# POOL waits at every eighth gather of a graph attention until the gathers before it have landed

## The reference, cut to what matters

```python
h = (x_flat @ W_gat).reshape(M, HEADS, NUM_EXPERTS)          # 4 heads x 4 experts
a_src = (h * att_src).sum(-1)
a_dst = (h * att_dst).sum(-1)
e = leaky_relu(a_src[src] + a_dst[dst], negative_slope=0.2)
ee = exp(e - segment_max(e, dst)[dst])
denom = segment_sum(ee, dst)
agg = segment_sum(h[src] * (ee / denom[dst])[:, :, None], dst) + b_gat
scores = _layernorm(agg, ln_gamma, ln_beta).reshape(M, HEADS, NUM_EXPERTS).mean(1)
topk_s, topk_i = top_k(scores, 2)
w = softmax(topk_s)
out = sum over ei of gate(ei) * (gelu(x @ W1[ei] + b1[ei]) @ W2[ei] + b2[ei])
```

## Time and profile before

| | |
|---|---|
| timed runs | 4308.76, 4301.39 and 4308.22 us, median 4308.22 us |
| profiled execution | span 4665.5 us from the first to the last instruction; no time of its own is given beside it |
| PE busy | 3696.0 us (79%) |
| DVE busy | 2192.7 us (47%) |
| ACT busy | 1348.5 us (29%) |
| POOL busy | 739.5 us (16%) |
| mean granted clock of PE | 0.886 |

### The profile page before, as it was taken

The page is one execution under the profiler, slowest core; times in us unless marked ns, Lnnn a source line. Parts: engine busy times, 40 slices in busy tenths (PEclk is TensorE's granted clock), DMA queues, the critical chain, the costliest instruction groups (busy, mean ns, idle before and its releaser), DMA issues. The chain is left out here.

```text
span 4665.5 us, 90783 instructions
## 1 busy us (share of the span) xinstructions
PE 3696.0 (79%) x23366; PEld 2634.7 (56%) x23367; DVE 2192.7 (47%) x5709; ACT 1348.5 (29%) x2983; POOL 739.5 (16%) x1224
## 2 busy tenths in 40 slices
PE   4888864899699989973464629859989899789998
PEld 2444433566388579651354416539879544457776
DVE  7888878888700221151263420270130677723333
ACT  2555532677700110320010203240000135233333
POOL 3222100000000000017423470200000466100000
PEclk9999975887799899986787859879999999989999
DMA  2111220323244024102010121224425100010000
GB/s 105 47 74 74 93 86 0 91 90 90 76 160 157 32 108 184 60 16 53 11 53 4 40 25 39 98 77 170 165 105 196 49 1 1 5 29 7 13 13 27
DMA packets 125733, 317.98 MB, mean 68 GB/s; under 512 B 43522, under 2 KB 76785, under 8 KB 111116
## 3 DMA queue, kind: packets, MB, share of 16 engines
q1 hardware_dynamic: 110404, 300.31, 18.5%
q0 software_dynamic: 11808, 9.68, 1.5%
q10 hardware_dynamic: 3404, 6.53, 0.4%
HBM read 244.21 MB, written 72.41 MB: 68 GB/s over the span
## 5 line engine op out<-in xcount | busy, mean ns | idle before, releaser
L554 PE MATMUL ps<-hot_key,hot_src 128*126 128x512 bf16 (+1 forms) x2208 | 416.9, 314 | 38.6 <-DVE hot_key L519 21.1
L519 DVE TENSOR_SCALAR hot_key<-col_iota,run_keys 128x625 bf16<-128x625 int16 x1104 | 393.7, 378 | 0.0
L2441 PE MATMUL ps<-xnT,ew 128*128 (+2 forms) x640 | 207.5, 479 | 206.7 <-issue 150.9
L1335 PE MATMUL ps<-gnn_u_thirds,near 125*128 125x256 bf16 x3000 | 334.7, 274 | 23.1 <-issue 23.1
L554 PEld LDWEIGHTS ps<-hot_key,hot_src 128*126 128x126 bf16 x2208 | 212.7, 136 | 234.2 <-DVE hot_key L519 171.7
L1335 PEld LDWEIGHTS ps<-gnn_u_thirds,near 125*128 125x128 bf16 x3000 | 329.7, 141 | 26.3 <-issue 24.7
L2441 PEld LDWEIGHTS ps<-xnT,ew 128*128 128x128 f32 x640 | 129.7, 210 | 279.2 <-issue 183.5
L2322 POOL DMA_INDIRECT rows_room<-node_table,src_idx x256 | 260.1, 1016 | 142.4 <-issue 142.4
L516 DVE TENSOR_SCALAR hot_src<-col_iota,run_srcs 128x125 bf16<-128x125 int16 x828 | 211.6, 256 | 97.4 <-PE ps L554 52.8
L863 PE MATMUL ps<-row_hot,slot_hot 128*128 128x512 f16 x1088 | 217.6, 351 | 3.1 <-DVE row_hot L1076 2.6
L2477 PE MATMUL ps<-table_thirds,rows_room 125*128 125x144 bf16 x1728 | 129.2, 232 | 113.9 <-issue 78.0
(11 more groups left out here) (570 smaller groups left out, 6651.9 us busy)
## 6 DMA issues: line engine op xcount, KB each, us to landing
near<-adjacency SPq DMA_DIRECT2D x80, 1562.5 KB, 6.6
adjacency<-counts SPq DMA_DIRECT2D x125, 312.5 KB, 2.2
own_in<-own_rows SPq DMA_DIRECT2D x34, 512.0 KB, 4.0
expert_rows<-rows_y SPq DMA_DIRECT2D x75, 125.0 KB
rows_room<-expert_rows SPq DMA_DIRECT2D x25, 375.0 KB
pair_in<-high_rows SPq DMA_DIRECT2D x34, 256.0 KB
pair_in<-low_rows SPq DMA_DIRECT2D x34, 256.0 KB
agg0a_adj<-adjacency SPq DMA_DIRECT2D x5, 1562.5 KB, 9.4
```

Of the source, the lines that this page charges most:

```text
L519: nc.vector.tensor_scalar(hot_key[:, j, :], col_iota[:], run_keys[:, ds(at, 1), j:j + 1].rearrange("p a j -> p (a j)"), None, ALU.is_equal ...
L554: last = nc.tensor.matmul(sums[:, b:e], hot_src[:, j, :], hot_key[:, j, b:e], start=False, stop=True, skip_group_check=True)
L1335: last = nc.tensor.matmul(ps[:, j, 0:width], lead_tiles[BUF[j]][:, k, :], parts.thirds[:, k, i, :], start=(k == 0 and i == 0), stop=(k == ...
L2441: last = nc.tensor.matmul(ps[:, piece % 2, 0:n], w1[i][:, c, m * 128:(m + 1) * 128], xnT[:, c, ds(g * NG + first, n)], start=(c == 0), sto ...
```

## The change

In `gather_rows`, ahead of every eighth gather of a call, POOL waits until all gathers that it has issued so far into this buffer have landed: 16 for each gather, plus what earlier blocks in the same buffer have added (`landed_before`). A buffer's very first gather (slot 96 in blocks 0 and 1, slot 0 in the others) is left out. The gathers, their order and everything else stay.

```diff
+                        def start_of(q):
+                            return TURNED if q < 2 else 0
+
+                        def landed_before(b, q):
+
+                            return 0 if q < 2 else (b - q) * (8 * SLOTS)
+
                         def gather_rows(b, q, first, stop):
 
                             alone(pool, idx_ready, b + 1)
                             for j in range(first, stop):
+                                if (j - first) % FEW == 0 and j > start_of(q):
+                                    alone(pool, got[q], landed_before(b, q) + 16 * (j - start_of(q)))
                                 pool.indirect_dma_start(
                                     out=fetched[q][:, j, :], out_offset=None, in_=node_table,
                                     in_offset=bass.IndirectOffsetOnAxis(ap=src_idx[:, q, j:j + 1], axis=0),
```

## The result

The kernel before takes 4308.49 us (median of four runs; one of them, 6012.78 us, is left out of the comparison), the changed kernel 4375.19 us (4373.02 to 4381.57, four runs). The ratio of the comparison is 1.017, 95% interval 1.0158 to 1.0182: slower by under 2%, but clear of the noise. The profiled execution of the changed kernel is one of its timed runs, 4376.03 us with a span of 4374.3, so here the profile may be read for the time. That of before had a span of 4665.5 us.

What follows compares the result with a forecast made beforehand. The profile's slow issue beside POOL's gathers was taken as absent from timed runs, leaving POOL's chain almost bare at `weigh_last`. Waits of 59 us less 4 of cover added 55 to 4308: 4363 us, range 4306 to 4405.

Steps and rivals of the forecast that it cites:

- the sum: POOL's chain of gathers: 59 us added by the waits, less 4 us of cover, so ACT stands 55 us.
- The premise: Beside POOL's gathers: the profile's 385.9 us lost to slow issue on PE are hardly present in the timed runs.
- rival "faster": Beside the gathers: slow issue is in timed runs too and pauses give the others room; down to 4280 us, chance 0.10.
- 28.6 us: Rest left unexplained, around or elsewhere in the span: 4279.6 us without the losses against the timed median of 4308.2.
- The price of a wait: POOL ahead of every eighth gather: 1.8 us per bare wait, 32 bare, 59 us in all (43 to 111).
- POOL's chain end at 2550: POOL's gathers before the change, rebuilt without the losses: chain ends at 2550 us, with 16 us for stretched gathers.
- rival "dearer": POOL's waits: landings slow down beside stores of expert rows, 3.23 us a wait; 4415 us, chance 0.08.
- The cover: At `weigh_last` on ACT: PE's side at 2566.9 against block 3's `exp_in` at 2563 hides 4 us of waiting.
- my bound of 20: At `weigh_last`: cover of POOL's chain is 20 us if gathers are not stretched by DVE's work.
- PE's clean arrival: At `weigh_last` in expert 2's last run: PE's side arrives at 2566.9 without the 365.0 us lost before.
- the case's own range: Whole kernel: the forecast's main case, chance 0.70, lies between 4331 and 4400 us.
- The signs: Profile after: POOL's gaps 2.1 us at 36 places, span falling while timed runs rise; wrong if the timed median falls too.

Runs made afterwards that it cites:

- 44 waits: Against the kernel before (4309.14 us): waits ahead of every fourth gather in blocks 0 and 1, every eighth in blocks 2 and 3; 4402.13 us, ratio 1.0206.
- 76: Against the kernel before (4309.14 us): the wait stands ahead of every fourth gather in all blocks; 4477.40 us, ratio 1.0389.

## Why the prediction was right, and what in it was not

Forecast 4363, measured 4375.2, in the range of 4306 to 4405, and slower, as 0.78 of the chances said. Two things in this are luck: that the result was timed on the kind of chip on which the kernel before takes 4308 us (on the other kind the direction is wrong), and that two errors of the sum have opposite signs. By its steps:

**The premise, right where it was tested and wrong in general.** "The timed runs have hardly any of this loss" holds for the 4308 us runs. That it belongs to the recording, as I let the Trainium skill, NOTIFIC — the notification-queue block (7.1 and 10), suggest, is neither shown nor excluded. The 4309 chip's runs were recorded too, so recording alone doesn't bring it about, and no run here shows the block. But the slow traces are the ones that lack landing records (306 of 2048 against all of them), and no run was timed unrecorded. What is shown is that the loss goes with the chip, or with the session on it, in all of the 4 to 20 runs of a kernel there. On a 4690 chip my rival "faster" is what happens, by 4.5%, and its price was too small: I let it win 28.6 us only, as I had capped the loss by the time of that one chip. Its point, that it decides once 59 us of loss are in the timed runs, was sound in kind: the runs there are 4691.2 - 4309.1 = 382 us longer.

**The price of a wait, too low.** I took 1.8 us for each of 32 bare waits, 59 in all, between 43 and 111. From the first start of a gather to the last are 2643.6 - 2117.3 = 526.3 us after. Without waits I had POOL's chain end at 2550, so its last gather starts 2549 - 2109.2 = 439.8 after the first. By that the waits lengthened it by 86.5 us, 2.4 each. The other two kernels agree: 550.3 - 439.8 = 110.5 for 44 waits (2.5), 627.7 - 439.8 = 187.9 for 76 (2.5). The 439.8 is worked out, not measured, but the gaps themselves, added up over the waits, say the same: 84.5, 107.2 and 186.8 us above 0.30. They also show where I was wrong. The 15 waits of block 2 stand 29.8 us above the usual gap, 2.0 each, near my 1.8; the 15 of block 3 stand 43.1, 2.9 each, with gaps of 3.04 and 3.89 where I counted 0.30 + 1.8. That is the rival "dearer", for block 3 alone. The Trainium skill, DMA: Bandwidth & Descriptors (Anatomy of one DMA — SWDGE path), gave an estimate of 1.65 a wait; the traces say 2.4 to 2.5. That account is of one DMA by itself; the slow landings of block 3 come beside other transfers, which no run took away, so that these are the reason is not shown.

**The cover, too small.** I found 4 us. Chain and time against before differ by 86.5 - 66.7 = 19.8 us, with 44 waits by 110.5 - 93.0 = 17.5, with 76 by 187.9 - 168.3 = 19.6. Three kernels with one intercept: about 19 us of the lengthening are hidden, once, and beyond them the time follows POOL's chain one for one (40 waits more: chain +101.4, time +101.6). That it is close to my bound of 20 is chance: that bound left out the stretching of gathers, and the chain without its waits, 526.3 - 84.5 = 441.8, has it. By these numbers ACT's last stop ended in a run of before at 4309.1 - (4375.2 - 2658.2) = 2592.1 in the frame of the profile after, 17 us later than PE's clean arrival of 2566.9, which is 2575.0 in that frame (the gathers and PE's runs start 8.1 us later there). That would be most of the 28.6 us that I left unexplained. In the changed kernel PE's side has no such 17 us: ACT came to its last stop at 2658.15 - 61.33 = 2596.8, and without the 22.5 us of its earlier stops in this part that is 2574.3, PE's clean arrival. So either the pauses won these 17 us back, as in the rival "faster" and with a small rest of slow issue on a 4309 chip too, or the kernel before waits for something else there. This is worked out, not seen: only a profile of before on a 4309 chip would tell.

So the sum was 59 - 4 = 55 where it is 86.5 - 19.8 = 66.7. Two terms were off by 27.5 and 16, and partly made up for each other. Two smaller slips changed nothing: the digits of PE beside the gathers are 3 4 6 4 6 2 and not "0 to 4", and the upper end of the case's own range adds up to 32 x 2.8 + 3 x 1.5 = 94 and not 92.

**Where the time goes.** ACT stands 61.3 us at `weigh_last`, as I placed it (55), and "some us" at the `weigh` of block 2 were 83.8 - 61.3 = 22.5 with one more stop: PE's matmul of the next run waits 24.7 us for ACT there. I took it for swallowed; it is, since the last stop is shorter by as much.

**The signs.** Gaps above 2 us: yes. 33 of 36 named as landings. Span down while the time rises: yes (4665.5 to 4374.3 against 4308.5 to 4375.2), but hardly for the reason given: the profile before is of the slow kind and the profile after is not, so the two compare kinds of chips. "I am wrong if the timed median falls with the span": on a 4690 chip it does. The waits of blocks 0 and 1 alone gained 17 us, but on a 4690 chip; how slow they are on a 4309 chip, which is what this sign asked, was not measured.

**What stays open.** Shown: on a 4690 chip the other engines' issue fades over some 16 gathers without a pause; a stop of POOL's gathers, by a wait or by idle tiles, restores it; bounding the gathers in flight to 16 doesn't. Not shown: what it is that fills up, whether it comes of the recording, whether a stop works as such or by letting the gathers land, where some 18 of the 84.5 us are hidden, and why one chip in four (and the one of the result) doesn't have the slow issue.

## What to carry to other kernels

Time a change on more than one chip, or at least compare the profile's span with the timed runs: where they differ by 8%, as here, the profile may show another kind of chip than the one that was timed, and both can turn up. Missing landing records are a second sign of it. A wait that stops an engine's stream of indirect DMAs is to be priced by the landing beside the other traffic (2.5 us here), and counted from the point where that stream's chain meets the others, not from its first place. No version here wins on both kinds of chips: where the kernel before takes 4309 us it is the best, where it takes 4690 the waits at every eighth gather take 4.5% off, and at every sixteenth 1.8%.

## What was not expected of the hardware

- The same program on different chips takes 4309 or 4679 to 4692 us, with runs of one chip within 0.3% of their median (but for the one of 6012.78), and nearly the whole difference lies beside one kind of work (385.9 us counted in the profile before, against 382): indirect DMAs that POOL issues back to back every 1.30 us. The changed kernel takes 4375 and 4480.
- In such a stretch PE goes from 64 matmuls in 10 us to 16 in 43 at a granted clock of 0.50, while DMA engines are busy 11% and move 10 GB/s. All other engines together issue 1 instruction in a us.
- A pause of some 2.3 to 4 us for each eighth gather brings back 211 of the 317 us between 4692 and 4375, and it need not be a wait for DMA.
- Where the issue is slow, the trace keeps 306 of the 2048 landing records of 128 gathers, and 901 when POOL pauses at every eighth; where it isn't, it keeps all 2048.
